# Expert outputs scattered to token order, FFN moved into its own batch's round, first preparation reordered

## The chip, the cores and the metric

The kernel runs on one core of a Trainium2 chip. The time is the device time of one execution in microseconds. Three executions of the kernel before took 855.63, 857.69 and 858.66 us; their median, 857.69 us, is what a new time is compared with.

## The reference

Input x has 8 batches of 512 tokens with 128 features. Two layers follow one another. The parts that matter here:

```python
# each layer: x = x + s * silu(moe or ffn), both from the layernormed xn
# layer 0: s = attention(xn), and the mixture of experts
normed = layernorm(hidden)                     # xf: (4096, 128)
top_idx = argmax(xf @ router_w)                # one of 8 experts per token
w = where(top_idx == e, sigmoid(max logit), 0)
routed += (silu(xe @ g) * (xe @ u)) @ d        # xe = xf * w, per expert
shared = silu(xf @ sh_gate) * (xf @ sh_up) @ sh_down
return hidden + routed + shared
# layer 1: s = state space model, and the FFN
xv = silu(conv(x @ W_in) + conv_b)
dt, B, C = split(xv @ W_x)
delta = softplus(dt @ W_dt + b_dt)
h[t] = exp(delta*A) * h[t-1] + delta * B * xv  # 16 states, scan over 512 tokens
y = (sum_n h * C + xv * D) @ W_out
ffn = (silu(xn @ w_gate) * (xn @ w_up)) @ w_down
out = x + y * silu(ffn)
```

## The kernel before, in words

All arithmetic is float32. The program has four blocks, one after another, and in each block every engine has its own list of instructions in program order, with semaphores between the engines. PE is TensorE, DVE is VectorE, ACT is ScalarE, POOL is GpSimd, SP issues plain DMAs.

**Block 1** (lines 142 to 465) normalises the tokens, finds each token's expert and a place (`pos`) for it in a list of 40 tiles of 128 slots, sorted by expert.

**Block 2** (lines 468 to 940) is attention with the shared expert, batch by batch, while POOL scatters the scaled tokens `nf_all` into `xs_dram` by `pos` (line 556). Then come the experts: for each of the 40 slot tiles SP loads 128 rows (four buffers `xs_t`), PE turns them, multiplies with the expert's weights, ACT and DVE make the hidden values, and SP stores the output tile `yt` to `ys_dram` (line 547), in slot order.

**Block 3 starts at line 943.** POOL first gathers the expert outputs back in token order, 32 indirect DMAs of 128 rows, each added onto `res_all` (line 1076). For batch i, `gates(i)` on ACT takes silu of that sum, and `residual(i)` on DVE multiplies it with attention's output, adds x and takes statistics; `moments(g)`, `roots(g)` and `norms(g)` normalise a group of batches (`GROUPS`, line 984), and `turn(i)` and `turned(i)` transpose them into `xn1T_all`.

Then the state space model runs in rounds, one batch each (`rounds`, line 1024). Round b scans batch b: in eight steps q, ACT writes the decays `dA` into PSUM banks 0 to 3 (line 1323), POOL writes the drives `dbx` = B times du (line 1158), DVE scans (line 1571, two scans per q), PE multiplies the states with `W_out` into banks 6 and 7, and DVE (twelve states) or ACT and POOL (four states) scale with C and sum up (lines 1587, 1360, 1090). In the same round the next batch b+1 is prepared: `conv_gate`, `ssm`, skip, C rows, `dt`, softplus (ACT: abs, relu, exp, ln; POOL: the sums, delta and du), and its FFN (`ffn_up`, `ffn_tanh`, `ffn_hidden`, `ffn_down`, `gate_tanh`, `gate`), all through PSUM banks 4 and 5; `x_in` and `conv_silu` start on batch b+2. The output of batch b-1 is put together on POOL.

The rounds of batch -1 (no scan) are written out by hand as `first_preparation` on PE, ACT and DVE: batch 0's preparation with its FFN, mixed with the gates, residuals and turns of the batches that are still arriving. Round 7, the last with scans, prepares nothing.

Where a helper issues the matmuls, their line is 1178.

Of the kernel before, what the change touches and what calls it, by code (L numbers as in the profile page):

```python
# [5 lines left out]
def attention_moe_mamba_ffn(nc, t, out):  # L6
# [13 lines left out]
    ds = bass.ds  # L20
# [22 lines left out]
    with ctx:  # L43
# [7 lines left out]
        xs_dram = nc.dram_tensor("xs_dram", [SLOT_TILES * P, D], fp32, kind="Internal").ap()  # L51
        ys_dram = nc.dram_tensor("ys_dram", [SLOT_TILES * P, D], fp32, kind="Internal").ap()
# [7 lines left out]
        nf_all = sb("nf_all", [P, NT, D])  # L60
# [81 lines left out]
        with ExitStack() as ph:  # L142
# [8 lines left out]
            zeros = sb1("zeros", [P, SLOT_TILES * D // 4])  # L151
# [25 lines left out]
            s_zd = sem("p1_slots_zeroed")  # L177
            s_ones = sem("p1_bv_ones")
# [18 lines left out]
            def _(sp):  # L197
# [21 lines left out]
            def _(pool):  # L219
                nc.gpsimd.memset(eps[:, :], LN_EPS).then_inc(s_eps, 1)  # L220
                nc.gpsimd.memset(bvb[:, :], 1.0).then_inc(s_ones, 1)
                nc.gpsimd.memset(zeros[:, :], 0.0).then_inc(s_zero, 1)
# [70 lines left out]
            def _(act):  # L293
# [23 lines left out]
                def scaled(b):  # L317
                    act.wait_ge(S["score"], b + 1)
                    act.wait_ge(S["nf_ps"], b + 1)
                    for i in tiles(b):  # L320
                        ins = nc.scalar.activation(nf_all[:, i, :], bank[bN[b % 2]][:, cols4(i)], ACT.Copy,
                                                   scale=score[:, i:i + 1])
# [23 lines left out]
            def _(dve):  # L346
# [59 lines left out]
                nc.vector.tensor_tensor(vobias[:, :], bank[bV][:, 0:D], rows[:, 0, :], ALU.add).then_inc(s_vob, 1)  # L406
                dve.wait_ge(s_std, 2)
# [60 lines left out]
        with ExitStack() as ph:  # L468
# [30 lines left out]
            xs_t = over[:, 0:UN * D].rearrange("p (u d) -> p u d", d=D)  # L499
# [5 lines left out]
            yt = over[:, 2560:2560 + UN * D].rearrange("p (u d) -> p u d", d=D)  # L505
            E = {n: sem("p4_" + n) for n in ("xT_ps", "xT", "gu_ps", "th", "ha", "hm", "hT_ps", "hT", "y_ps", "y")}
            s_in = [sem(f"p4_slots_loaded_{i}") for i in range(UN)]
            s_out = [sem(f"p4_slots_stored_{i}") for i in range(UN)]
# [9 lines left out]
            def _(sp):  # L518
# [14 lines left out]
                for u in range(UN):  # L533
# [14 lines left out]
                for u in range(UN):  # L548
                    sp.wait_ge(s_out[u], 16 * (SLOT_TILES // UN))
# [1150 lines left out]
```

## Time and profile before

| | |
|---|---|
| median of 3 executions | 857.69 us (855.63 to 858.66) |
| the profiled execution | 858.88 us |
| its span, first to last instruction | 857.0 us |
| PE, DVE, ACT, POOL busy | 674.9, 674.2, 485.3, 516.6 us |
| mean granted clock of TensorE | 0.928 of full speed |

The span is 1.9 us shorter than the execution's own time. Busy times are sums of instructions; a wait on a semaphore or the issue of a DMA from SP is not busy. A row of the timeline merges instructions of one kind that follow one another (x4: four of them). "Idle before" is how long the engine had stood, and the arrow names what ended it. The granted clock is 1.0 at 2.4 GHz and 0.5 at 1.2 GHz.

### The profile page before, as it was taken

Reading aid. Unit: us, or ns where it says so; the run is one execution under the profiler, and the core shown is the slowest. Engines: PE = TensorE matmul, PEld = TensorE weight load, DVE = VectorE, ACT = ScalarE, POOL = GpSimd, SP = SyncE. Lnnn points to the kernel's source line nnn. Section 1 sums busy time; section 2 is a strip of 40 time slices with the busy share of each in tenths; the row PEclk is TensorE's granted clock in tenths of the full one; section 3 lists DMA queues with packets and bytes.
Section 4 is the critical chain, followed back from the end, with each engine's and each line's share of the span. In section 5 each row is a group of like instructions: output and inputs, shape, how many; then the busy total and the mean of one; then the engine's idle time right before and its main releaser. Section 6 shows DMA issues by size and latency. Waiting matters only on the chain. (4 is left out here: it accounts for less than half of the span.)

```text
span 857.0 us, 13505 instructions
## 1 busy us (share of the span) xinstructions
PE 674.9 (79%) x3984; PEld 499.7 (58%) x3984; DVE 674.2 (79%) x1174; ACT 485.3 (57%) x946; POOL 516.6 (60%) x281
## 2 busy tenths in 40 slices
PE   1948999998999614335889899898798897988573
PEld 1934656665555401213577787777677776778573
DVE  6855786876666434274999999989999999999994
ACT  1625666665434223151785875956858668586561
POOL 1006610000000088662489999999899999999993
PEclk9968999999999956675999999999999999999998
DMA  7501100001222123520211320413203213142000
GB/s 220 199 10 47 44 15 0 0 12 55 56 64 68 47 31 37 130 98 0 100 50 50 117 71 27 161 50 109 77 26 135 74 42 136 34 137 75 12 2 13
DMA packets 45062, 56.41 MB, mean 66 GB/s; under 512 B 6344, under 2 KB 35536, under 8 KB 45008
## 3 DMA queue, kind: packets, MB, share of 16 engines
q1 hardware_dynamic: 37648, 51.00, 18.3%
q0 software_dynamic: 5632, 4.20, 2.7%
q10 hardware_dynamic: 1728, 0.57, 0.3%
q8 instruction: 24, 0.39, 0.2%
q14 instruction: 30, 0.25, 0.1%
HBM read 46.06 MB, written 9.70 MB: 65 GB/s over the span
## 5 line engine op out<-in xcount | busy, mean ns | idle before, releaser
L1571 DVE TENSOR_TENSOR_SCAN xnT_all<-psum,nfT_all 128x1024 f32<-128x1024 f32 x128 | 285.3, 2269 | 2.7 <-issue 2.7
L1178 PEld LDWEIGHTS psum<-W_out,xnT_all 128*128 128x128 f32 x2048 | 242.4, 196 | 40.4 <-issue 38.5
L1178 PE MATMUL psum<-W_out,xnT_all 128*128 128x128 f32 x2048 | 244.9, 279 | 18.7 <-DVE acc L1587 18.7
L1323 ACT ACTIVATE psum<-delta,A 128x511 f32<-128x511 f32 x256 | 163.2, 678 | 40.1 <-DVE xnT_all L1571 39.3
L1076 POOL DMA_INDIRECT res_all<-ys_dram,pos x32 | 50.3, 1572 | 196.3 <-issue 196.3
L1158 POOL TENSOR_TENSOR nfT_all<-nf_all,du 128x1024 f32<-128x1024 f32 x64 | 149.1, 2357 | 24.1 <-DVE xnT_all L1571 22.9
L1158 POOL TENSOR_TENSOR nfT_all<-attn_all,du 128x1024 f32<-128x1024 f32 x64 | 149.6, 2360 | 4.0 <-DVE xnT_all L1571 4.0
L1587 DVE SCALAR_TENSOR_TENSOR acc<-psum,Cc,acc 128x128 f32<-128x128 f32 x352 | 96.5, 339 | 7.8 <-PE psum L1178 7.8
L1178 PE MATMUL psum<-vo_all,wgu 128*128 128x512 f32 (+1 forms) x96 | 51.2, 660 | 43.9 <-DVE hff L1607 43.7
L556 POOL DMA_INDIRECT xs_dram<-nf_all,pos x32 | 31.9, 996 | 68.3 <-issue 57.5
L1178 PE MATMUL psum<-vo_all,W_taps 128*128 (+4 forms) x128 | 59.9, 615 | 0.7 <-ACT vo_all L1341 0.7
L1178 PEld LDWEIGHTS psum<-vo_all,wgu 128*128 128x128 f32 x96 | 17.1, 198 | 60.4 <-issue 46.8
L605 PEld LDWEIGHTS psum<-vo_all,PT 128*128 128x128 f32 x256 | 31.0, 191 | 23.5 <-ACT PT L750 17.6
L669 PE MATMUL psum<-gud,xnT_all 128*128 x80 | 43.6, 628 | 0.4 <-ACT xnT_all L785 0.4
L1360 ACT ACTIVATE ts<-psum,Cc 128x128 f32<-128x128 f32 x128 | 35.7, 356 | 10.1 <-PE psum L1178 10.1
L1178 PEld LDWEIGHTS psum<-vo_all,W_taps 128*128 128x128 f32 x128 | 24.4, 200 | 26.5 <-issue 25.4
L605 PE MATMUL psum<-vo_all,PT 128*128 (+1 forms) x256 | 36.9, 287 | 1.4 <-ACT PT L750 1.4
L909 DVE COPY xnT_all<-psum 128x256 f32<-128x256 f32 x40 | 17.0, 424 | 26.0 <-PE psum L681 26.0
L575 PE MATMUL psum<-k_w,q_w 128*128 128x512 f32 x64 | 34.4, 624 | 0.8 <-issue 0.8
L1603 DVE SCALAR_TENSOR_TENSOR fa<-tf,psum 128x512 f32<-128x512 f32 x24 | 15.9, 661 | 23.8 <-ACT tf L1371 23.8
L1178 PE MATMUL psum<-wd,hff 128*128 128x128 f32 x192 | 26.1, 298 | 9.4 <-DVE hff L1607 9.4
L1347 ACT ACTIVATE tconv<-psum,convb 128x512 f32<-128x512 f32 x16 | 10.9, 684 | 37.6 <-PE psum L1178 37.6
(189 smaller groups left out, 1163.7 us busy)
## 6 DMA issues: line engine op xcount, KB each, us to landing
nf_all<-bt_dram SPq DMA_DIRECT2D x32, 512.0 KB, 5.3
attn_all<-bt_dram SPq DMA_DIRECT2D x32, 512.0 KB, 3.6
xs_dram<-zeros SPq DMA_DIRECT2D x4, 640.0 KB, 7.5
xnT_all<-xs_dram SPq DMA_DIRECT2D x40, 64.0 KB, 1.9
ys_dram<-xnT_all SPq DMA_DIRECT2D x40, 64.0 KB, 1.5
x_all<-in_x_dram SPq DMA_DIRECT2D x8, 256.0 KB, 6.2
out_dram<-ow SPq DMA_DIRECT2D x8, 256.0 KB, 2.4
gud<-in_gate_dram SPq DMA_DIRECT2D x1, 1024.0 KB, 6.7
```

Of the source, the lines that this page charges most:

```text
L556: pool.indirect_dma_start(xs_dram, bass.IndirectOffsetOnAxis(ap=pos[:, i:i + 1], axis=0), nf_all[:, i, :], None).then_inc(s_sc, 16)
L575: nc.tensor.matmul(bank[j % 2], q_w[:, j * P:(j + 1) * P], k_w[:, :], start=True, stop=True)\
L605: ins = nc.tensor.matmul(bank[4][:, j * P:(j + 1) * P], PT[:, j % 2, c, :], vo_all[:, ds(b * TPB + c, 1), :], start=(c == 0), stop=(c == T ...
L669: nc.tensor.matmul(bank[2 + u % 2], xT[:, u % 2, :], gud_flat[:, ds(expert[u], 2 * I)], start=True, stop=True).then_inc(E["gu_ps"], 1)
L909: nc.vector.tensor_copy(hT[:, u % 2, :, :], bank[4 + u % 2][:, 0:KI * P].rearrange("p (k s) -> p k s", s=P))\
L1076: pool.indirect_dma_start(res_all[:, i, :], None, ys_dram, bass.IndirectOffsetOnAxis(ap=pos[:, i:i + 1], axis=0), compute_op=ALU.add).then ...
L1158: nc.gpsimd.tensor_tensor(dbx[:, i % R, :, :], B_pair(q), du[:, p, h:h + 1, :].to_broadcast([P, 2, L]), ALU.mult)\
L1178: return nc.tensor.matmul(o, l, r, start=start, stop=stop)
L1323: ins = nc.scalar.activation(dA[:, i % RA, k, 1:L], delta[:, p, h, 1:L], ACT.Exp, scale=A[:, h, 2 * q + k:2 * q + k + 1])
L1360: ins = nc.scalar.activation(ts[:, i, j, :], bank[Gb[n % 2]][:, j * P:(j + 1) * P], ACT.Copy, scale=Cc[:, p, j, n:n + 1])
L1571: nc.vector.tensor_tensor_scan(hring[:, i % R, :, :].rearrange("p n l -> p (n l)"), dA[:, i % RA, :, :].rearrange("p n l -> p (n l)"), dbx ...
L1587: nc.vector.scalar_tensor_tensor(acc[:, p, j, :], bank[Gb[m % 2]][:, j * P:(j + 1) * P], Cc[:, p, j, m:m + 1], acc[:, p, j, :] if i else s ...
```

## The change

**Experts' outputs.** A token's row in `xs_dram` gets a 129th word, its token number, written in block 1 (`token`, into the last column of `nf_rows`); the rows that fill up unused slots carry numbers of spare rows behind the last token. The output tiles are no longer stored by SP but scattered by POOL with these numbers into `moe_dram`, in token order, within the experts' stage. Block 3 then reads a batch's 512 rows with one plain DMA that adds onto `res_all`: 8 DMAs in place of 32 gathers. `xs_t` has eight buffers; the load of tile u+8 waits for the scatter of tile u.

**FFN.** All steps of batch b's FFN move from round b-1 to round b. The round before the first scan has none, and the last round gets one.

**First preparation.** On PE, ACT and DVE it is written in another order. Skip, C rows and the two dt products use banks 0 to 3, which hold the decays later (`bS, bC, bD`), so the zero columns of `dA` are set after them. The two softplus sums, delta and du of batch 0 move from POOL to DVE. The groups of batches are (0), (1, 2), (3 to 7) in place of (0), (1 to 3), (4 to 7); the variance takes six DVE operations in place of eight; silu's table is loaded ahead.

```diff
@@ block 1
+                link(nc.vector.tensor_scalar(token[:, :], thr, pid[:, 0:1], None, ALU.add))
+                nc.vector.tensor_copy(nf_rows[:, :, D].bitcast(u32), token[:, :])
...
@@ experts, SP
-                for u in range(SLOT_TILES):
-                    if u + UN < SLOT_TILES:
-                        sp.wait_ge(E["xT_ps"], u + 1)
-                        sp.dma_start(xs_t[:, u % UN, :], slots(xs_dram, u + UN)).then_inc(s_in[u % UN], 16)
-                    sp.wait_ge(E["y"], u + 1)
-                    sp.dma_start(slots(ys_dram, u), yt[:, u % UN, :]).then_inc(s_out[u % UN], 16)
...
+                for u in range(SLOT_TILES - XN):
+                    sp.wait_ge(E["xT_ps"], u + 1)
+                    sp.wait_ge(s_out[u % UN], 16 * (u // UN + 1))
+                    sp.dma_start(xs_t[:, u % XN, :], slots(xs_dram, u + XN)).then_inc(s_in[u % XN], 16)
@@ experts, POOL
+                for u in range(SLOT_TILES):
+                    pool.wait_ge(E["y"], u + 1)
+                    pool.wait_ge(s_in[u % XN], 16 * (u // XN + 1))
+                    pool.indirect_dma_start(moe_dram, bass.IndirectOffsetOnAxis(ap=xs_t[:, u % XN, D:ROW].bitcast(u32), axis=0),
+                                            yt[:, u % UN, :], None).then_inc(s_out[u % UN], 16)
@@ block 3, POOL
-                    for i in range(b * TPB, (b + 1) * TPB):
-                        pool.indirect_dma_start(res_all[:, i, :], None, ys_dram,
-                                                bass.IndirectOffsetOnAxis(ap=pos[:, i:i + 1], axis=0),
-                                                compute_op=ALU.add).then_inc(s_moe[b % 2], 16)
+                    pool.dma_start(res_all[:, b * TPB:(b + 1) * TPB, :],
+                                   moe_dram[b * L:(b + 1) * L, :].rearrange("(j p) d -> p j d", p=P),
+                                   accum_op=ALU.add).then_inc(s_moe[b % 2], 16)
@@ PE, first_preparation
                         ssm()
-                        skip()
-                        C_rows()
                         dt(0)
                         dt(1)
                         turn(1)
                         turn(2)
-                        ffn_up(0)
+                        skip()
+                        C_rows()
+                        pe.wait_ge(F["xT"], 2)
+                        x_in(b + 2, 0)
                         turn(3)
-                        ffn_up(1)
-                        ffn_up(2)
-                        ffn_down()
-                        x_in(b + 2, 0)
+                        turn(4)
                         x_in(b + 2, 1)
...
@@ DVE, rounds
-                        if prep and 3 <= q < 6:
+                        if scan and 3 <= q < 6:
                             ffn_hidden(q - 3)
...
-                        if prep and q == 6:
+                        if scan and q == 6:
                             gate()
```

How the instructions of an engine stand in the program, at the places that the prediction speaks of. In the names, `nf_all` and `nf_rows` are the same memory, which in block 3 holds B broadcast to all partitions.

POOL at the start of block 3, before (the gathers are all 32 of line 1076; here the first twelve and the last four), then the first preparation's sums:

```order
L1076 DMA res_all<-ys_dram,pos 128x128 x8
L1076 DMA res_all<-ys_dram,pos 128x128 [waits p5_gathered_0]
L1076 DMA res_all<-ys_dram,pos 128x128 x3
...
L1115 TENSOR_TENSOR lg<-lg,rl 128x1024 [waits p6_delta,p6_lg,p6_rl]
L1119 TENSOR_TENSOR e<-ab,e 128x1024 [waits p6_e1]
L1127 TENSOR_TENSOR delta<-e,lg 128x1024 [waits p6_dA,p6_du,p6_corr,p6_sp]
L1135 TENSOR_TENSOR du<-delta,xv 128x1024 [waits p6_dbx,p6_xv,p6_delta]
L1158 TENSOR_TENSOR nfT_all<-nf_all,du 128x1024 [waits p6_scan,p6_B_loaded_0,p6_du]
```

and now, from the last of the experts' scatters (`moe_dram` with `xnT_all`'s part `yt`) on:

```order
L575 DMA moe_dram<-xnT_all 5376x128 [waits p4_slots_loaded_7,p4_y]
...
L1095 DMA res_all<-moe_dram 128x4x128 x2
L1095 DMA res_all<-moe_dram 128x4x128 [waits p5_gathered_0]
L1095 DMA res_all<-moe_dram 128x4x128 [waits p5_gathered_1]
...
L1177 TENSOR_TENSOR nfT_all<-nf_rows,du 128x1024 [waits p6_scan,p6_B_loaded_0,p6_du]
```

The sums of batch 0 have left POOL, and its first work on data is the drives. DVE before the first scan, before (`fa`, `hff`, `G`: the FFN; `ts`: the normed rows):

```order
L1540 TENSOR_SCALAR var<-var 128x16 [waits p5_mv]
L1603 SCALAR_TENSOR_TENSOR fa<-tf,psum 128x512 [waits p6_hf,p6_tf]
L1607 SCALAR_TENSOR_TENSOR hff<-fa,psum 128x512 [waits p6_dn_ps,p6_fa]
...
L1613 SCALAR_TENSOR_TENSOR G<-tg,psum 128x512 [waits p6_og,p6_tg]
L1545 RECIPROCAL rs<-std 128x16 [waits p5_std]
L1552 TENSOR_SCALAR ts<-x_all,mean,rs 128x128 [waits p5_xT_ps,p5_rs]
```

and now:

```order
L1563 SCALAR_TENSOR_TENSOR var<-tmp,var 128x20 [waits p5_mv]
L1633 TENSOR_TENSOR lg<-lg,rl 128x1024 [waits p6_rl,p6_lg]
L1637 TENSOR_TENSOR e<-ab,e 128x1024 [waits p6_e1]
L1628 MEMSET psum 128x4 [waits p6_rl,p6_acc0,p6_C]
L1642 TENSOR_TENSOR delta<-e,lg 128x1024 [waits p6_corr,p6_sp]
L1647 TENSOR_TENSOR du<-delta,xv 128x1024 [waits p6_delta]
L1569 RECIPROCAL rs<-std 128x20 [waits p5_std]
L1576 TENSOR_SCALAR ts<-x_all,mean,rs 128x128 [waits p5_rs]
L1576 TENSOR_SCALAR ts<-x_all,mean,rs 128x128 x3
```

Four operations came in, three pairs of the FFN and its gate went out, and the last group of norms has 20 operations in place of 16. The third place is DVE in the last round, before, where a scan's pair is followed by sums alone:

```order
L1571 SCALAR_TENSOR_TENSOR xnT_all<-psum,nfT_all 128x1024 [waits p6_G,p6_dbx,p6_dA] x2
L1587 SCALAR_TENSOR_TENSOR acc<-psum,Cc,acc 128x128 [waits p6_acc,p6_G]
L1587 SCALAR_TENSOR_TENSOR acc<-psum,Cc,acc 128x128 [waits p6_acc] x3
L1571 SCALAR_TENSOR_TENSOR xnT_all<-psum,nfT_all 128x1024 [waits p6_G,p6_dbx,p6_dA] x2
L1587 SCALAR_TENSOR_TENSOR acc<-psum,Cc,acc 128x128 [waits p6_acc,p6_G]
```

and now, in the steps 3 to 5 (the gate follows in step 6):

```order
L1595 SCALAR_TENSOR_TENSOR xnT_all<-psum,nfT_all 128x1024 [waits p6_G,p6_dbx,p6_dA] x2
L1653 SCALAR_TENSOR_TENSOR fa<-tf,psum 128x512 [waits p6_hf,p6_tf]
L1657 SCALAR_TENSOR_TENSOR hff<-fa,psum 128x512 [waits p6_dn_ps,p6_fa]
L1611 SCALAR_TENSOR_TENSOR acc<-psum,Cc,acc 128x128 [waits p6_acc,p6_G]
L1611 SCALAR_TENSOR_TENSOR acc<-psum,Cc,acc 128x128 [waits p6_acc] x3
```

In the other rounds the FFN's operations stand where they stood, with another batch's number in their waits.

## Rows read from the trace of the kernel before

**Rows 1.** Busy time by stage: us, then PE, PEld, DVE, ACT, POOL, clock, DMA share, GB/s

```profile
212.00:296.00 84.00, 77.03 (x360) 45.57 (x360) 51.76 (x134) 33.26 (x121) 0.00 (x0) 1.00 0.22 61
...
296.00:417.00 121.00, 46.05 (x128) 23.72 (x128) 58.07 (x122) 42.65 (x59) 72.73 (x42) 0.65 0.25 53
...
694.00:749.00 55.00, 50.32 (x338) 40.36 (x337) 53.66 (x76) 39.95 (x72) 54.18 (x27) 1.00 0.25 83
...
803.00:857.00 54.00, 31.89 (x256) 30.57 (x255) 42.67 (x62) 20.91 (x44) 39.25 (x22) 0.93 0.03 10
...
304.00:336.00 32.00, 10.52 (x20) 4.60 (x20) 12.70 (x43) 9.69 (x12) 26.60 (x18) 0.61 0.29 35
```

**Rows 2.** Timeline of POOL, 300 to 361 us: start, duration, instruction, idle before

```profile
300.44 1.62 POOL L1076 DMA_INDIRECT res_all<-ys_dram,pos  x1 [186.84 <-issue]
...
306.06 1.54 POOL L1076 DMA_INDIRECT res_all<-ys_dram,pos  x1 [0.30 <-issue]
...
358.66 1.54 POOL L1076 DMA_INDIRECT res_all<-ys_dram,pos  x1 [0.30 <-issue]
```

**Rows 3.** Timeline of ACT, 300 to 400 us

```profile
309.37 1.28 ACT L1331 ACT_TABLE_LOAD   x1 [14.71 <-DMA res_all<-ys_dram,pos]
...
337.97 0.69 ACT L1347 ACTIVATE tconv<-psum,convb 128x512 f32<-128x512 f32 x1
...
358.43 0.63 ACT L1331 ACTIVATE xnT_all<-res_all 128x512 f32<-128x512 f32 x1 [10.18 <-DMA res_all<-ys_dram,pos]
...
366.51 1.28 ACT L1400 ACT_TABLE_LOAD   x1
...
367.80 1.06 ACT L1400 ACTIVATE ab<-ab 128x1024 f32<-128x1024 f32 x1
...
397.34 0.60 ACT L1371 ACTIVATE tf<-psum 128x512 f32<-128x512 f32 x1 [20.70 <-PE psum L1178]
```

**Rows 4.** Timeline of DVE, 330 to 420 us

```profile
332.42 0.69 DVE L1519 TENSOR_TENSOR xnT_all<-xnT_all,attn_all 128x512 f32<-128x512 f32 x1 [5.08 <-ACT xnT_all L1331]
...
340.25 3.16 DVE L1552 TENSOR_SCALAR ts<-x_all,mean,rs 128x128 f32<-128x128 f32 x12
...
382.79 0.18 DVE L137 TENSOR_TENSOR tmp<-tmp 128x16 f32<-128x16 f32 x1
...
389.83 2.26 DVE L1540 TENSOR_SCALAR var<-var 128x16 f32<-128x16 f32 x1
...
411.51 4.46 DVE L1571 TENSOR_TENSOR_SCAN xnT_all<-psum,nfT_all 128x1024 f32<-128x1024 f32 x2
...
417.14 4.47 DVE L1571 TENSOR_TENSOR_SCAN xnT_all<-psum,nfT_all 128x1024 f32<-128x1024 f32 x2
```

**Rows 5.** Timeline of POOL beside attention, one of the scatters

```profile
76.94 0.95 POOL L556 DMA_INDIRECT xs_dram<-nf_all,pos  x1 [1.53 <-DMA xs_dram<-nf_all,pos]
```

**Rows 6.** Waits in the experts' stage, 212 to 296 us: total, times, longest

```profile
PE psum L655 <- DMA xnT_all<-xs_dram: 2.0, 4, 0.8
```

**Rows 7.** Timeline of PE, 316 to 365 us

```profile
317.00 1.08 PE L1301 MATMUL psum<-const,ts 128*128 128x128 f32 x4 [22.65 <-DVE ts L1552]
...
318.77 9.44 PE L1178 MATMUL psum<-vo_all,W_taps 128*128 128x512 f32 x16 [0.69 <-ACT vo_all L1341]
...
340.13 3.63 PE L1178 MATMUL psum<-xv,W_x 128*40 128x512 f32 x4 [11.92 <-DVE xv L1597]
...
360.56 3.62 PE L1178 MATMUL psum<-ssmT,W_dt 128*128 128x512 f32 x4
```

**Rows 8.** Timeline of POOL, 382 to 393 us

```profile
382.79 9.27 POOL L1158 TENSOR_TENSOR nfT_all<-nf_all,du 128x1024 f32<-128x1024 f32 x4
```

**Rows 9.** Timeline of DVE, 767 to 791 us, a round's FFN

```profile
767.68 0.65 DVE L1603 SCALAR_TENSOR_TENSOR fa<-tf,psum 128x512 f32<-128x512 f32 x1
...
768.37 0.69 DVE L1607 SCALAR_TENSOR_TENSOR hff<-fa,psum 128x512 f32<-128x512 f32 x1
...
790.14 0.68 DVE L1613 SCALAR_TENSOR_TENSOR G<-tg,psum 128x512 f32<-128x512 f32 x1
```

More of the change, by code:

```diff
@@ L532, in _ @@
                 sp.wait_ge(s_sc, NT * 16)
-                for u in range(UN):
+                for u in range(XN):
                     sp.dma_start(xs_t[:, u, :], slots(xs_dram, u)).then_inc(s_in[u], 16)
@@ L989, in attention_moe_mamba_ffn @@
             rs1 = sb6("rs1", [P, NT])
+            eps1 = sb6("eps1", [P, 1])
             over = xnT_all[:, :]
@@ L1231, in dt @@
                         w("ssm", 1)
-                        if h:
+                        if h and scan:
                             w("C", 1)
-                        mm(bank[bM[h]], W_dt[:, h * P:(h + 1) * P], ssmT[:, :]).then_inc(S["dt_ps"], 1)
+                        mm(bank[bD[h]], W_dt[:, h * P:(h + 1) * P], ssmT[:, :]).then_inc(S["dt_ps"], 1)
                     def skip():
@@ L1451, in first_preparation @@
                         conv_silu(b + 2, 0)
+                        turned(3)
+                        turned(4)
                         conv_silu(b + 2, 1)
-                        for i in GROUPS[2]:
-                            turned(i)
+                        turned(5)
+                        turned(6)
+                        turned(7)
                     if prep and not scan:
@@ L1465, in round_ @@
                             scale_state(b, p, q - 3)
+                        if scan and 2 <= q < 5:
+                            ffn_tanh(q - 2)
+                        if scan and q == 5:
+                            gate_tanh()
                         if not prep:
@@ L1499, in _ @@
                 gates(3)
+                gates(4)
                 conv_silu(0, 0)
+                gates(5)
+                conv_silu(0, 1)
+                gates(6)
+                gates(7)
                 roots(1)
-                conv_silu(0, 1)
-                gates(4)
-                gates(5)
                 rounds(act, round_)
@@ L1590, in add_state, with conv_gate @@
                                                            ALU.mult, ALU.add).then_inc(S["acc"], 1)
[L1592 to L1598 removed]
+                    def conv_gate(h):
+                        if h == 0:
+                            w("acc_ps", 0)
+                            w("du", 0)
+                        w("yh", h + 1)
+                        nc.vector.scalar_tensor_tensor(xv[:, h, :], tc_[:, h, :], 1.0, bank[bM[h]],
+                                                       ALU.add, ALU.mult).then_inc(S["xv"], 1)
@@ new lines, in deltas, with drives @@
+                    def deltas():
+                        w("sp", 1)
+                        w("corr", 1)
+                        nc.vector.tensor_tensor(delta[:, 1 - p, :, :], e1[:, :, :], lg[:, :, :], ALU.add)\
+                            .then_inc(S["delta"], 1)
+                    def drives():
+                        w("delta", 1)
+                        nc.vector.tensor_tensor(du[:, 1 - p, :, :], delta[:, 1 - p, :, :], xv[:, :, :], ALU.mult)\
+                            .then_inc(S["du"], 1)
```

204 lines of the change are left out of this document (111 added, 93 removed).

## The prediction

> **What bounds the kernel now.** I read the stages first, then inside the one that no engine fills, engine by engine. The experts' stage (212 to 296) is PE's. The rounds (694 to 749) are DVE's and POOL's, with 53.7 and 54.2 us busy of 55; the last one (803 to 857) is lighter, since it prepares no next batch [rows 1]. Between them lie 121 us (296 to 417) in which DVE is busy 58 us and PE 46 us at 0.65 of its clock: a chain of waits, not work.
>
> In that stretch POOL issues 32 gathers from 300.4 to 360.2, one each 1.88 us [rows 2]. ACT works in program order, so its gate of batch 6 at 358.4 waits 10.2 us for a gather while the skip, the C rows and the softplus stand behind it [rows 3]. After that the shared FFN is in the way: its second tanh runs at 397.3 after 20.7 us of waiting [rows 3], because DVE was in small variance operations of 2.2 us each. The first scan starts at 411.5, the third at 417.1 [rows 4]. From there on the rounds repeat, so I follow the change to the third scan and then only to the end.
>
> **Part 1, before the experts.** Seven small DVE operations give the row numbers; one of such size takes 0.18 us [rows 4], with gaps 1.2 us in all, on DVE's path: +1.2. Rows of 516 B in place of 512 are scattered beside attention, whose scatters had some 100 us of room: 0.
>
> **Part 2, the experts' stage.** The store of each slot leaves SP and becomes an indirect scatter on POOL, which was idle there. A scatter takes 0.95 us, its pause 0.3, and it lands 1.5 later [rows 5]; a slot's step takes about 2.0 us (some 80 us for 40), and four output buffers give 8 us, so POOL keeps up and nobody waits for it. On SP the refill is no longer behind a store, and eight buffers replace four: it now waits for the scatter of the same slot (2.5 us after the output), with over three steps to spare. PE waited 2.0 us for loads, four times [rows 6]; with the irregular step behind each I take 3.0 back. The last scatter's issue is 0.6 longer than a store's (0.95 against some 0.35). POOL, which started at 300.4 [rows 2], starts at 300.4 + 1.2 - 3.0 + 0.6 = 299.2.
>
> **Part 3, the residual's input.** 32 gathers become eight plain accumulating DMAs of 256 KB. No row shows one. From below: the issue of one gather, 1.54 us, while the bytes need at least 2.2 us (35 GB/s kept 0.29 of the DMA engines busy [rows 1], so 121 GB/s is the most). From above: the same cost per row as a gather, 4 x 1.54 = 6.2 us. I take 3.0, nearer the lower end, because the rows need no index, and the gather's price contains one. A landing comes 1.8 us after an issue's end (307.6 [rows 2] to 309.4 [rows 3]), so batch 0 is there at t0 = 299.2 + 3.0 + 1.8 = 304.0. Up to 2.9 us a batch the chain below never waits for batch 7, needed at t0 + 20.4; at 3.0 it hardly does.
>
> The Trainium skill, DMA: Bandwidth & Descriptors, section Anatomy of one DMA, gives 2.0 us plus the bytes at 436 GB/s for such a DMA and calls descriptor generation small; by it t0 would be about 301.8, and the sum 2.2 us less. No row here has a direct one.
>
> **Part 4, the chain from t0 to the third scan.** All from rows; PE at its low level, since it idles between.
> - Gate, residual, variance, norm, turn: 9.4 us before (309.4 [rows 3] to 318.8 [rows 7]); less a table load moved ahead (1.28 [rows 3]) and two links of DVE, 7.6.
> - x_in, both halves: 9.4 [rows 7]. To t0 + 17.0.
> - conv_silu's two passes 1.4 [rows 3] and the gate's product 0.7 [rows 4]: 19.0.
> - ssm 3.6 [rows 7], copied out 0.6 [rows 3]: 23.3. The gates of 3 to 7 and their residuals (2.3 us each) fit on ACT and DVE beside x_in.
> - Both dt 3.6 [rows 7] and the second abs and relu 1.4: 28.2.
> - Exp, Ln, each with a table load, 2 x 2.35 [rows 3], then two passes of 1.06: 35.0.
> - ACT goes on with skip, C and two turned copies, then root and its table, until 38.5. DVE makes the sum, delta and du, no longer POOL: 128x1024 with two SBUF inputs is 1.2 us (0.69 for 512 columns, 0.18 for 16 [rows 4]), so three of them after ACT's last pass: 38.6. POOL had taken about 2.4 for each.
> - Now DVE has norms(2), 20 tensor_scalars (0.26 each, twelve in 3.2 [rows 4]), 5.3 us, and POOL starts four products of B and du, 9.3 us [rows 8], at the same moment. While those four ran before, a DVE operation over 16 columns took 2.26 us instead of 0.18 [rows 4], one per POOL operation. So I add the two: 14.6, and norms(2) ends at 53.2.
> - The first scan starts then. The third waits for a row of work on PE and ACT behind batch 4's norms (about 49): a turn 1.1 [rows 7], x_in's second half 4.7, conv_silu 1.4, the last turn with its copy and a bank's wait 2.5, two decays 1.3. Third scan at t0 + 60.0 = 364.0.
>
> Before it was 417.1, so this saves 53.1. Batch 0's FFN is not on this chain any more.
>
> **Part 5, the rounds.** FFN of batch b moves from round b-1 to round b, in the same slots; seven rounds hold one FFN as before. The last round gets one that it did not have. DVE is full there, so all of its work counts: 3 x (0.65 + 0.69) + 0.68 [rows 9] = 4.7 us. PE and ACT have room for theirs in a round with a full DVE, and do the same in the rounds before. The tail behind the last scan stays.
>
> **Sum.** 857.0 - 53.1 + 4.7 = 808.6 us of span. The profiled execution took 858.88 for 857.0 of span, 1.9 more: 810.5. The median of the runs, 857.69, is 1.2 below that execution; I forecast **809.5 us**. About 0.3%, 2.6 us, is what a measurement of this kernel can tell from no change.
>
> **The rivals.**
> - *The DMAs cost by the row* (6.2 us a batch). t0 is 3.2 later, and batch 7 comes 43.4 us after batch 0, not 20.4 at the latest: 23.0 more. 809.5 + 26.2 = 835.7. For it: scatter and gather both are priced 128 rows at a time, 0.95 and 1.54. Against: an index is part of both. Chance 0.2; a pitch of 4 to 5 us gives 817 to 826 and is in my case.
> - *DVE is not held by POOL in norms(2)*. Then it ends at 43.9, and the third scan is bound by x_in and the turns at about t0 + 54.3: 803.8. For it: twelve norms ran at 0.26 while gathers were issued. Against: those write descriptors only, and the row of 2.26 is itself a tensor_scalar. Chance 0.1.
> - *The scatters hold the experts*, which ends slower than before. POOL takes one slot after another; as soon as a scatter with its pause needs more than 2.0 us, every step takes that long, and from 2.0 + 48/40 = 3.2 us the whole gain is gone. At two gathers' issues and a pause, 3.4 us, it is 40 x 1.4 = 56 more: 866. Against: 32 scatters took 0.95 beside a DVE that was busy with one- and two-input operations [rows 5]. Chance 0.03.
> - *The FFN in the last round costs nothing or the shorter preparation is eaten in round 0*: the first would need DVE to idle there, and it doesn't; the second would need round 0 to lack something (B loads come 7 us after ssm, in time). Up to 10 us more, 0.04, inside the range.
>
> The Trainium skill, SBUF — State Buffer, section SBUF: two separate sides, says for the third rival that a DVE operation in a 2-port mode keeps GpSimd from writing descriptors, 3.1 us in place of 0.62 for such a DMA. By that rule the step would be at its edge, 3.1 to 3.4 us, and the time near 860. It would need such operations in the loop; the loop's three DVE operations read PSUM, and no row shows a scatter held.
>
> **How the numbers follow.** My case with its slower pitches, 801 to 826, has 0.65; the case by the row 0.2; DVE unheld 0.1; the rest slower still. The low end takes in DVE unheld together with the earlier t0, 800. The high end reaches a pitch of 5.7 us, 832. Faster by over 0.3%: 0.96, since even the case by the row is 22 us faster. Slower: 0.03. Same: 0.01.
>
> **What would show it.** In the profile after: POOL has 40 scatters between about 217 and 297 at 1 us; eight DMAs end by 325; the first scan starts near 357 and the third near 364, with DVE's norms(2) at 2.3 us for the first few of them; DVE shows fa, hff and G in the last round, which grows by 4.7 us. I am wrong in the size if POOL's eight issues last over 3 us each, or if ACT waits for a DMA after the gate of batch 2; wrong in the mechanism if the third scan is early but the rounds after it are longer than the 55 us of before; wrong in the sign only if the experts' stage grows from 84 us to over 130.

## The result, and the profile after

The changed kernel takes 814.1 us (median of 4 runs, 812.6 to 815.2) against 856.7 us before (854.9 to 858.7): ratio 0.950, 95% interval 0.947 to 0.953, so 5% faster. The forecast was 809.5 with a range of about 800 to 832. In the profiled executions the span went from 857.0 to 811.8 us, 45.2 less; the sum of the prediction had 48.4.

Busy time by stage, with the columns of [rows 1] (experts, preparation, round 0, round 6, last round with the end):

```profile
212.00:292.00 80.00, 75.85 (x358) 45.21 (x358) 51.26 (x133) 32.94 (x120) 38.06 (x40) 1.00 0.21 60
300.00:365.00 65.00, 31.83 (x94) 16.00 (x95) 49.46 (x115) 37.26 (x54) 24.08 (x14) 0.74 0.45 98
363.00:419.00 56.00, 50.36 (x327) 39.30 (x327) 52.04 (x70) 39.94 (x68) 46.17 (x21) 0.97 0.22 76
695.00:750.00 55.00, 46.81 (x328) 40.57 (x327) 53.58 (x76) 37.89 (x67) 54.26 (x27) 0.94 0.25 83
750.00:812.00 62.00, 42.26 (x300) 37.05 (x298) 48.45 (x73) 24.24 (x50) 40.39 (x23) 0.88 0.03 9
```

Between the experts and the third scan lie 74 us (291 to 365) where 121 had been, and in the last 65 of them DVE is busy 49. POOL has 38 us of work in the experts' stage and nobody waits for it. The row for 694 to 749 in [rows 1] is round 5, so round 6 is compared by its third scans: 53.8 us from 697.2 to 751.0 now, 53.5 from 749.1 to 802.6 before. From the last round's third scan to the end there are 60.8 us where 54.4 had been. Timeline of POOL, the end of the experts and the residual's input:

```profile
291.40 0.96 POOL L575 DMA_INDIRECT moe_dram<-xnT_all  x1 [0.78 <-ACT xnT_all L817]
303.96 2.76 POOL L1095 DMA_DIRECT2D res_all<-moe_dram  x2 [11.60 <-issue]
308.81 1.28 POOL L1095 DMA_DIRECT2D res_all<-moe_dram  x1 [2.09 <-DMA res_all<-moe_dram]
...
320.22 1.28 POOL L1095 DMA_DIRECT2D res_all<-moe_dram  x1 [0.59 <-DMA res_all<-moe_dram]
```

Against [rows 2]: eight issues of 1.3 to 1.4 us in place of 32 of 1.54, the last over at 321.5. But the first starts at 303.96, later than the first gather did (300.44). POOL's last scatter was issued by 292.4; then 11.6 us pass. Timeline of ACT:

```profile
290.85 0.28 ACT L817 ACTIVATE xnT_all<-psum 128x128 f32<-128x128 f32 x1 [1.46 <-PE psum L712]
300.11 1.28 ACT L1333 ACT_TABLE_LOAD   x1 [8.98 <-PEq L483]
...
308.54 0.63 ACT L1351 ACTIVATE xnT_all<-res_all 128x512 f32<-128x512 f32 x1 [6.94 <-DMA res_all<-moe_dram]
...
335.46 1.06 ACT L1422 ACTIVATE ab<-ab 128x1024 f32<-128x1024 f32 x1
```

From the end of the last output's copy (291.13) to block 3's first instruction 9.0 us go by. Before the change it was 2.2, from 294.66 to 296.88, by the timelines of ACT and DVE of the kernel before:

```profile
294.38 0.28 ACT L798 ACTIVATE xnT_all<-psum 128x128 f32<-128x128 f32 x1 [1.46 <-PE psum L693]
...
296.88 0.48 DVE L1509 MEMSET ssmT<- 128x512 f32 x1 [3.53 <-PEq L468]
```

The gate of batch 0, 308.54, is the prediction's t0. The softplus's exp runs at t0 + 27. Timeline of DVE after the change:

```profile
343.54 1.23 DVE L1647 TENSOR_TENSOR du<-delta,xv 128x1024 f32<-128x1024 f32 x1
...
344.99 13.30 DVE L1576 TENSOR_SCALAR ts<-x_all,mean,rs 128x128 f32<-128x128 f32 x20
358.21 4.46 DVE L1595 TENSOR_TENSOR_SCAN xnT_all<-psum,nfT_all 128x1024 f32<-128x1024 f32 x2
...
364.90 4.47 DVE L1595 TENSOR_TENSOR_SCAN xnT_all<-psum,nfT_all 128x1024 f32<-128x1024 f32 x2 [1.05 <-ACT psum L1343]
371.33 1.13 DVE L1611 SCALAR_TENSOR_TENSOR acc<-psum,Cc,skip_sb 128x128 f32<-128x128 f32 x4 [1.97 <-PE psum L1192]
```

The third scan came at 417.1 [rows 4] and now comes at 364.9, 52.2 us earlier. The norms took 13.3 us for 20 (forecast 14.6). Timeline of PE:

```profile
315.96 8.99 PE L1192 MATMUL psum<-vo_all,W_taps 128*128 128x512 f32 x16 [0.69 <-ACT vo_all L1361]
327.14 1.91 PE L1192 MATMUL psum<-xv,W_x 128*40 128x512 f32 x4 [2.20 <-DVE xv L1621]
330.56 1.98 PE L1192 MATMUL psum<-ssmT,W_dt 128*128 128x512 f32 x4 [1.51 <-ACT ssmT L1399]
...
363.99 3.47 PE L1192 MATMUL psum<-xv,W_x 128*40 128x512 f32 x4 [0.95 <-DVE xv L1621]
...
796.93 5.44 PE L1192 MATMUL psum<-W_out,xnT_all 128*128 128x128 f32 x32 [3.49 <-DVE acc L1611]
```

The ssm and dt of batch 0 run at a granted clock of 1.00 (1.91 and 1.98 us), where [rows 7] has 3.6 each at 0.50. PE had idled 2.20 and 1.51 us before them, and 11.92 before that ssm of the kernel before. The last two lines show the opposite: the ssm of round 0 at 0.52 and the last projections at 0.69. The same work before, both at 1.00:

```profile
417.29 1.88 PE L1178 MATMUL psum<-xv,W_x 128*40 128x512 f32 x4 [2.01 <-DVE xv L1597]
...
843.66 3.81 PE L1178 MATMUL psum<-W_out,xnT_all 128*128 128x128 f32 x32 [2.62 <-DVE acc L1587]
```

### The profile page after: what moved, and what is told of

It reads as the page before. It is cut to its first block and busy times, and to the rows that moved or that the text cites. A ratio compares the mean times of both kernels' runs of the same rounds, so it can differ in the third digit from the quotient of the medians.

```text
span 811.8 us, 13548 instructions
## 1 busy us (share of the span) xinstructions
PE 667.7 (82%) x3984; PEld 495.1 (61%) x3984; DVE 671.3 (83%) x1180; ACT 482.2 (59%) x944; POOL 504.8 (62%) x293
## 5 line engine op out<-in xcount | busy, mean ns | idle before, releaser
L1177 POOL TENSOR_TENSOR nfT_all<-nf_rows,du 128x1024 f32<-128x1024 f32 x64 | 149.3, 2362 | 33.0 <-DVE du L1647 23.3
L575 POOL DMA_INDIRECT moe_dram<-xnT_all x40 | 38.4, 960 | 141.3 <-ACT xnT_all L817 141.3
L568 POOL DMA_INDIRECT xs_dram<-nf_rows,pos x32 | 31.4, 981 | 68.1 <-issue 56.1
L1192 PE MATMUL psum<-vo_all,wgu 128*128 128x512 f32 (+1 forms) x96 | 48.2, 625 | 26.8 <-DVE hff L1657 26.8
L1192 PE MATMUL psum<-vo_all,W_taps 128*128 (+4 forms) x128 | 62.4, 635 | 7.1 <-ACT vo_all L1361 7.1
L624 PEld LDWEIGHTS psum<-vo_all,PT 128*128 128x128 f32 x256 | 31.0, 191 | 23.6 <-ACT PT L769 17.6
L1380 ACT ACTIVATE ts<-psum,Cc 128x128 f32<-128x128 f32 x128 | 35.8, 359 | 13.4 <-PE psum L1192 13.2
L1109 POOL TENSOR_TENSOR accP<-accP,ts 128x512 f32<-128x512 f32 x16 | 20.4, 1272 | 18.0 <-ACT ts L1380 18.0
L1321 PE MATMUL psum<-const,ts 128*128 128x128 f32 x32 | 5.9, 333 | 30.6 <-DVE ts L1576 29.4
```

The lines of the kernel that those rows point to most:

```text
L568: pool.indirect_dma_start(xs_dram, bass.IndirectOffsetOnAxis(ap=pos[:, i:i + 1], axis=0), nf_rows[:, i, :], None).then_inc(s_sc, 16)
L575: pool.indirect_dma_start(moe_dram, bass.IndirectOffsetOnAxis(ap=xs_t[:, u % XN, D:ROW].bitcast(u32), axis=0), yt[:, u % UN, :], None).the ...
L624: ins = nc.tensor.matmul(bank[4][:, j * P:(j + 1) * P], PT[:, j % 2, c, :], vo_all[:, ds(b * TPB + c, 1), :], start=(c == 0), stop=(c == T ...
L1109: nc.gpsimd.tensor_tensor(accP[:, :, :], ts[:, 0, :, :] if i == 1 else accP[:, :, :], ts[:, i, :, :], ALU.add).then_inc(S["accP"], 2 if i ...
L1177: nc.gpsimd.tensor_tensor(dbx[:, i % R, :, :], B_pair(q), du[:, p, h:h + 1, :].to_broadcast([P, 2, L]), ALU.mult)\
L1192: return nc.tensor.matmul(o, l, r, start=start, stop=stop)
```

## The experiments

**The parts alone.** Three kernels take the change apart. The first has the scatters and the plain DMAs only:

```diff
-sp.dma_start(slots(ys_dram, u), yt[:, u % UN, :]).then_inc(s_out[u % UN], 16)
+pool.indirect_dma_start(moe_dram, bass.IndirectOffsetOnAxis(ap=xs_t[:, u % XN, D:ROW].bitcast(u32), axis=0),
+                        yt[:, u % UN, :], None).then_inc(s_out[u % UN], 16)
...
-    pool.indirect_dma_start(res_all[:, i, :], None, ys_dram,
+pool.dma_start(res_all[:, b * TPB:(b + 1) * TPB, :],
```

> The kernel before with the scatters to token order and the eight plain DMAs alone; the FFN and the first preparation stay as they were. Theory: the path of before waits for gathers at the gates of batches 3 to 6, so block 3's start moves little, the ssm that started at 340.1 comes near 329 and the second dt's abs that ended at 365.5 comes near 338; the FFN in the way stays as long as it was. The third scan, 417.1 before, comes near 390, and the time near 830 us. Rival: the waits behind the FFN (20.7 us at its second tanh) swallow the earlier start, third scan after 405 and the time above 845.

Measured 834.1 us, ratio 0.972 (0.970 to 0.975). Timeline of its DVE:

```profile
390.00 4.47 DVE L1589 TENSOR_TENSOR_SCAN xnT_all<-psum,nfT_all 128x1024 f32<-128x1024 f32 x2
397.49 1.13 DVE L1605 SCALAR_TENSOR_TENSOR acc<-psum,Cc,skip_sb 128x128 f32<-128x128 f32 x4 [3.02 <-PE psum L1196]
```

The third scan is where the theory put it, 27.1 us earlier, but the median is only 23.6 lower. Round 0 accounts for 1.6 of the difference (57.2 us from third scan to third scan for 55.6): its ssm took 3.40 us instead of 1.88, and DVE's first accumulation waited 3.0 us for PE instead of 1.4. Another 1.2 is that the profiled execution of the kernel before, whose 417.1 is compared, ran 1.2 above its median; the rest is below 1 us.

The second kernel has the rest: the FFN and the preparation as changed, the gathers as before.

> The changed kernel with the old gathers: SP stores the slots, 32 indirect gathers fill the residual's input; FFN and preparation as changed. Theory: the last gather lands near 362, ACT's ssm copy now stands behind the gate of batch 7, so the softplus starts near 370, the first scan near 395 and the third near 401; with 4.7 us for the last round's FFN the time is near 846 us. So both parts alone give 27 and 11 us, together 43: the gathers hide half of what the new order gives. Rival: the parts add up, this one gives 16 us or more, time under 841.

Measured 846.5 us, ratio 0.987 (0.984 to 0.990), third scan at 397.4 (401 expected). The two parts give 23.6 and 11.2 us, 34.8 together, and the whole change 42.6. The third kernel moves the FFN alone (`ffn_up`, `ffn_tanh`, `ffn_hidden`, `gate` count b in place of b + 1, and go out of the first preparation).

> The kernel before with the FFN of each batch moved to the round of its own scans and nothing else. Theory (DVE's norms are held one per POOL operation while POOL's softplus sums and products run): third scan near 400 in place of 417.1, last round 4.7 longer, time near 845 us. If the norms are not held: third scan near 391, time 836. Rival: the FFN in the preparation cost nothing because something else ends at the same time, then the time is 857.7 + 4.7 = 862.

Measured 846.9 us, ratio 0.986 (0.983 to 0.990). Timeline of its DVE:

```profile
373.79 16.91 DVE L1547 TENSOR_SCALAR ts<-x_all,mean,rs 128x128 f32<-128x128 f32 x16
390.63 4.45 DVE L1566 TENSOR_TENSOR_SCAN xnT_all<-psum,nfT_all 128x1024 f32<-128x1024 f32 x2
...
396.19 4.45 DVE L1566 TENSOR_TENSOR_SCAN xnT_all<-psum,nfT_all 128x1024 f32<-128x1024 f32 x2
```

Sixteen norms took 16.9 us beside POOL's sums and products, and 4.2 before the change, when POOL was idle:

```profile
407.40 4.19 DVE L1552 TENSOR_SCALAR ts<-x_all,mean,rs 128x128 f32<-128x128 f32 x16
```

So the case with the norms held is the one that holds. The FFN alone gives as much as FFN and preparation together do while the gathers are there (10.8 and 11.2): behind late input the reordered preparation earns nothing that these times resolve. No kernel has the scatters and the FFN without it, so how much of the 7.8 us by which the whole exceeds its parts belongs to the preparation, and how much to the FFN alone, is not shown.

**The end of the experts' block.** The 9.0 us after the last output were in no term of the prediction. First, POOL issues the DMAs of batches 0 and 1 in the experts' block, behind its wait for the last scatters:

```diff
 for u in range(UN): pool.wait_ge(s_out[u], 16 * (SLOT_TILES // UN))
+pool.wait_ge(S["res"], at(NB - 1, "res", 1))
+for b in range(2):
+    pool.dma_start(res_all[:, b * TPB:(b + 1) * TPB, :],
+                   moe_dram[b * L:(b + 1) * L, :].rearrange("(j p) d -> p j d", p=P),
+                   accum_op=ALU.add).then_inc(s_moe[b % 2], 16)
...
-for b in range(NB):
+for b in range(2, NB):
```

> The changed kernel, with POOL issuing the plain DMAs of batches 0 and 1 in the experts' block, right behind its wait for the last scatters. From the last output (290.9) to block 3's first instruction 9 us pass, 2.2 before the change. Theory: the scatters' semaphores are there by 293.5 and the end of POOL's block costs the rest; the two DMAs are then issued at 293.5 to 296.3, the block ends 6 to 7 us behind the last of them (near 303), and the gate of batch 0 runs at block 3's start, 303 to 304 in place of 308.5; time 809 us. Rival: the last scatters land late; the DMAs are issued only at 299 to 300, the block ends at 303 without a further wait, the gate at 304 to 305.

```profile
292.70 0.96 POOL L576 DMA_INDIRECT moe_dram<-xnT_all  x1 [0.78 <-ACT xnT_all L823]
295.64 2.75 POOL L582 DMA_DIRECT2D res_all<-moe_dram  x2 [1.98 <-DMA moe_dram<-xnT_all]
309.10 2.58 POOL L1099 DMA_DIRECT2D res_all<-moe_dram  x2 [10.70 <-issue]
```

POOL's timeline settles the first question: the scatters' semaphores are there 2.0 us after the end of the last issue, so the landing is not what is late. But the block then ended at 305.3, 6.9 us after the two DMAs' issue, and the gate ran at 306.7, not at 303 to 304. 813.1 us, ratio 0.949 (0.946 to 0.952): not distinguishable from the changed kernel. The theory was right that the landing is not the cause and wrong about the gain: the end of the block moved back with the two DMAs.

Then the kernel before with additional indirect scatters by POOL: one behind the last output (its edit is shown), one behind the 28th (the number 28 in place of 40), and one behind each of the 40 with a single wait behind them all.

```diff
+pool.wait_ge(E["y"], 40)
+pool.indirect_dma_start(aside, bass.IndirectOffsetOnAxis(ap=pos[:, 0:1], axis=0), vo_all[:, 0, :], None).then_inc(s_aside, 16)
+pool.wait_ge(s_aside, 16)
```

> The kernel before with one more indirect scatter of 128 rows by POOL behind the last expert output, to a tensor that nobody reads. Theory: a scatter shortly before the end of POOL's block makes that end 6 to 7 us late: from the last output to block 3's first instruction 9 us in place of 2.2, as in the changed kernel, and the time near 864. Rival: the scatter's own issue and landing (0.7 + 1.0 + 1.5 us) is all: 3.5 us from the output, time near 859.

> The same, with the added scatter behind the 28th output, some 24 us before the last. Theory: what costs is the short time since the last scatter; POOL's end of block is over long before the other engines' and the time is that of before, 857. Rival: the cost is paid at the common end whenever POOL issued an indirect DMA late in the block: time near 863.

> The kernel before with 40 more indirect scatters of 128 rows by POOL, one behind each expert output, to tensors that nobody reads (nothing of the kernel itself is left out). With one such scatter behind the last output, block 3's first instruction came 2.6 us after its landing (6.3 after the last output); in the changed kernel, with 40, 5.8 us after (9.0 after the last output). Theory: the end of POOL's block grows with the number of indirect DMAs issued in it, 72 here as in the changed kernel: 9.0 us from the last output. Rival: it is something else of the changed kernel (longer rows, other waits on SP), and this one shows 6.3 again.

The last output's copy (ACT) ended at 291.64, 293.35 and 295.68. Block 3's first instruction (DVE) in each of the three, one behind the last, one behind the 28th, and 40:

```profile
297.98 0.48 DVE L1515 MEMSET ssmT<- 128x512 f32 x1 [7.66 <-PEq L469]
```

```profile
295.59 0.48 DVE L1515 MEMSET ssmT<- 128x512 f32 x1 [3.56 <-PEq L469]
```

```profile
304.73 0.48 DVE L1516 MEMSET ssmT<- 128x512 f32 x1 [10.36 <-PEq L469]
```

That is 6.3, 2.2 and 9.0 us. One scatter just before the end costs 4.1 us more than none (by the 2.0 us above it had landed 3.7 us after the output); one that is 24 us old costs nothing; 40 make it 9.0, the same as in the changed kernel, with none of its other edits. So the unexpected 6.8 us belong to the scatters on POOL, not to row length or SP's waits. Each of the three kernels was executed once: 858.1, 857.7 and 869.5 us. The forecast 864 for the first was too high by 6. In that execution the experts' first copy came 3.4 us earlier (209.2 against 212.6, ahead of any edit) and the experts took 0.4 more, so that block 3 began only 1.1 later than before; its third scan was yet 2.5 earlier (414.6 against 417.1), which was not explained. What happens in the microseconds before block 3 was not resolved; the trace of the changed kernel shows no instruction and no DMA traffic between 293.3 and 300.1.

The other part of the gap is POOL's own: it gives out its semaphore increments ahead of the first DMA.

```diff
-for n, per in names.items(): pool.sem_inc(S[n], 2 * per)
 for b in range(NB):
+    if b == 2:
+        for n, per in names.items(): pool.sem_inc(S[n], 2 * per)
```

> The changed kernel, with POOL issuing the first two plain DMAs ahead of its 40-odd semaphore increments in block 3. Theory: the increments take the 3.8 us between the block's start (300.1) and the first DMA (304.0), so the first DMA is at 300.2, the gate of batch 0 at 304.8, and the whole chain behind it 3.7 us earlier: 810.4 us. Rival: some engine waits for an increment in that time, or the gap is the block's entry on POOL and stays: within 1 us of 814.

```profile
300.44 2.75 POOL L1095 DMA_DIRECT2D res_all<-moe_dram  x2 [8.24 <-POOLq L483]
305.25 1.28 POOL L1095 DMA_DIRECT2D res_all<-moe_dram  x1 [2.06 <-DMA res_all<-moe_dram]
```

The gate of batch 0 came at 304.99 and the median 809.8 us, ratio 0.945 (0.942 to 0.947). So 3.5 us of the chain were 39 increments, instructions that count as no work in a profile. The whole chain did not keep them. DVE's timeline has the first scan 3.6 us earlier and the third 2.0:

```profile
362.92 4.47 DVE L1595 TENSOR_TENSOR_SCAN xnT_all<-psum,nfT_all 128x1024 f32<-128x1024 f32 x2 [2.42 <-ACT psum L1343]
```

That scan waited 2.4 us for ACT's decays, behind the second half of x_in, which took 5.74 us on PE where it had taken 4.16. The ssm that follows then took 1.91 us for 3.47, and round 0 was 54.3 us for 56.2 (third scan to third scan).

**The norms beside POOL.** POOL waits for all norms before its first product of round 0:

```diff
 pool.wait_ge(S["du"], at(b, "du", 1))
+if not end: pool.wait_ge(F["xn"], NB)
```

> The changed kernel, with POOL waiting for all of DVE's norms before its first product of B and du in round 0. Theory: the 20 tensor_scalars that took 13.3 us beside four POOL products take 0.26 each, 5.3 in all, when POOL is idle; the first scan comes at 352.6 in place of 358.2 and the third near 358.5 in place of 364.9; time 808 us. Rival A: the norms are slow by themselves (their inputs or outputs), they still take 13 us, and the time grows by 5 to 9 us. Rival B: the norms are faster, but POOL has lost its lead of products and round 0 becomes POOL's: it grows from 56.3 to 60 or more us and the time is within 2 us of 814.

```profile
344.82 5.21 DVE L1578 TENSOR_SCALAR ts<-x_all,mean,rs 128x128 f32<-128x128 f32 x20
...
352.62 4.61 DVE L1597 TENSOR_TENSOR_SCAN xnT_all<-psum,nfT_all 128x1024 f32<-128x1024 f32 x2 [2.58 <-issue]
...
358.32 4.46 DVE L1597 TENSOR_TENSOR_SCAN xnT_all<-psum,nfT_all 128x1024 f32<-128x1024 f32 x2
```

DVE's timeline has the same twenty operations in 5.2 us in place of 13.3, and the scans within 0.2 us of the forecast. Time 811.4 us, ratio 0.946 (0.942 to 0.950), an interval that overlaps the changed kernel's (0.947 to 0.953). By the profiled executions 3.5 of the 6.6 us are left; the rest came back as a longer round 0 and a longer round 3 (56.3 us for 54.7), where DVE waited 3.0 us for PE's projections in place of 1.4, behind an ssm of 3.51 us for 1.91. Rival B had the direction, but the round it gave 60 us has 57.0 (from conv gate to conv gate; 56.3 in the changed kernel).

The middle way lets POOL make one product first, together with the DMAs ahead of the increments:

```diff
 pool.wait_ge(S["scan"], at(b, "scan", i + 1 - R))
+if not end and i == 1: pool.wait_ge(F["xn"], NB)
```

> The changed kernel with two edits together: POOL issues the first two plain DMAs ahead of its semaphore increments, and in round 0 it makes one product of B and du, then waits for DVE's norms, then goes on. Theory: the gate of batch 0 is at 305.0, du ends near 341.3; one norm is held 2.3 us by the one product, the other 19 take 0.26 each, so the norms end at 348.7 and the first scan starts there; the third is near 357.5; POOL has one product more in hand than when it waited for all norms, so round 0 is no longer than 56.3. Time near 807. Rival: each product that POOL lacks at the first scan comes back as a wait in round 0 (57.0 there with none in hand), and the time stays at 809 to 810, what the first edit gave alone.

807.3 us, ratio 0.942 (0.940 to 0.944). DVE's timeline:

```profile
343.38 7.17 DVE L1578 TENSOR_SCALAR ts<-x_all,mean,rs 128x128 f32<-128x128 f32 x20
350.47 2.28 DVE L1597 TENSOR_TENSOR_SCAN xnT_all<-psum,nfT_all 128x1024 f32<-128x1024 f32 x1
...
356.52 4.46 DVE L1597 TENSOR_TENSOR_SCAN xnT_all<-psum,nfT_all 128x1024 f32<-128x1024 f32 x2
```

One product costs the norms one hold: 7.2 us. The chain up to du ran 1.9 us later than assumed, so the first scan came at 350.5 and not at 348.7; the third, 356.5, was 1.0 earlier than forecast. The last of this group keeps both edits and moves the norms of three batches to ScalarE:

```diff
+nc.vector.scalar_tensor_tensor(nm1[:, c], mean1[:, c], -1.0, rs1[:, c], ALU.mult, ALU.mult)
+nc.scalar.activation(xn1[:, i % 4, j, :], x_all[:, k, :], ACT.Identity, bias=nm1[:, k:k + 1], scale=rs1[:, k:k + 1])
```

> The same two edits, and the norms of batches 5 to 7 are made by ScalarE (x times the reciprocal root plus a bias that DVE computes), right behind its first decays; POOL waits after its first product for DVE's norms of batches 3 and 4 only. Theory: ScalarE is not held by POOL, 12 of its passes over 128 columns take 0.28 each as its output copies do; DVE's 8 norms end near 346, first scan 346, the third waits for ScalarE's copies and x_in's second half and comes near 356; time near 805. Rival: ScalarE becomes the bound of the stretch, the third scan comes after 358, and the time is that of the kernel with all norms on DVE or more.

807.2 us, ratio 0.941 (0.939 to 0.943), no better. DVE's timeline, then ACT's:

```profile
345.18 2.24 DVE L1589 SCALAR_TENSOR_TENSOR nm<-mean,rs 128x20 f32<-128x20 f32 x1
347.35 2.13 DVE L1598 TENSOR_SCALAR ts<-x_all,mean,rs 128x128 f32<-128x128 f32 x8
...
360.56 4.47 DVE L1617 TENSOR_TENSOR_SCAN xnT_all<-psum,nfT_all 128x1024 f32<-128x1024 f32 x2 [2.78 <-ACT psum L1347]
```

```profile
349.92 1.64 ACT L1369 ACTIVATE ts<-x_all,nm,rs 128x128 f32<-128x128 f32 x4
```

ScalarE needs 0.41 us a norm, not the 0.28 assumed, and the third scan waits for it and comes at 360.6, not 356: the rival's case. While it did so POOL was at work on its products (from 349.6 on). One operation over 20 columns was held for 2.24 us by POOL's product while eight norms without a product beside them took 2.13 together. The Trainium skill, SBUF — State Buffer, section SBUF: two separate sides, names which DVE operations contend with GpSimd for a shared port pair: those in a 2-port mode, and those with two SBUF inputs beside a GpSimd operation that reads SBUF; ScalarE never waits for it. The rows here agree as far as they go: the one held for 2.24 us has two SBUF inputs, and the scans, with one input in PSUM, take 2.27 to 2.29 us with POOL at work. The norms run from SBUF to SBUF and are held; that they do so in a 2-port mode is shown by no row.

**TensorE's clock.** The kernel with one product ahead of the norms (807.3 us), with work for PE that nobody reads in two gaps:

```diff
+for k in range(2): mm(bank[Gb[0]], ident, xn1T_all[:, 0:L])      # round 0, ahead of ssm
+for k in range(3): mm(bank[bM[0]], ident, xn1T_all[:, 0:L])      # last round, ahead of the last two projections
```

> The kernel with the two edits (DMAs ahead of the increments, one product ahead of the norms), and TensorE given work that nobody reads in two gaps: two matmuls over 512 columns (1.9 us) ahead of round 0's ssm, and three (2.8 us) ahead of the last two projections. Theory: in those places TensorE ran at its low level because it had idled before them: round 0's ssm took 3.3 to 3.6 us where TensorE was granted 0.52 and 1.9 where 1.0 was granted, and the last 32 matmul records 5.44 in every kernel with the FFN in the last round (idle 3.49 before) and 3.81 in those without (idle 2.62). With the gaps filled they take 1.9 and 3.8, round 0 is 1.5 shorter than 56.0 and the last part 1.6 shorter: time 804.5 us against 807.3. Rival: the added matmuls only push back the ssm and the projections, or the level stays low whatever runs there: time 807 to 809.

```profile
354.41 3.48 PE L1194 MATMUL psum<-vo_all,const 128*128 128x512 f32 x4 [0.69 <-ACT vo_all L1368]
357.83 2.06 PE L1194 MATMUL psum<-xv,W_x 128*40 128x512 f32 x4
...
787.27 2.74 PE L1194 MATMUL psum<-vo_all,const 128*128 128x512 f32 x6
790.92 3.81 PE L1194 MATMUL psum<-W_out,xnT_all 128*128 128x128 f32 x32 [0.91 <-DVE acc L1618]
```

805.7 us, ratio 0.940 (0.938 to 0.942). At the end the projections took 3.81 us as in the kernels without that round's FFN. The expectation says that every kernel with it showed 5.44, which is one too many: the kernel with norms on ScalarE idled 3.49 us there and took 3.81. So the 3.81 here fits the theory without proving it. In round 0 the added matmuls themselves ran low: the ssm started 1.8 us after the conv gates' end (356.0), where it had followed within 0.2, and though it then took 2.06, nothing was gained (a round of 56.45 us from conv gate to conv gate against 56.03). The end is 1.7 us shorter (59.1 us from the last round's third scan for 60.8), but round 3 is 1.6 longer (56.3 for 54.7), with its ssm at 2.93 us for 1.91, so the two profiled executions differ by 0.1 us (spans 804.1 and 804.2). The step over the kernel without them (0.942) is not resolved by the times; 1.0% over the changed kernel (0.950) is. This kernel has the lowest median of all the versions tried.

## Why the prediction was right, point by point

**Part 1 and 2, up to block 3.** The seven operations took 1.4 us (1.2 forecast). Where the experts start varies by 3.9 us between executions of the same code (first copy at 208.9 to 212.8 in six kernels that share it), which hides it. From the first slot's copy to the end of the last output's the old code needs 82.1 us in the trace of before (81.9 to 82.8 in the six) and the changed kernel 79.5, so 2.6 less for the 3.0 forecast; the waits of [rows 6] are gone. A scatter took 0.96 us for the 0.95 of [rows 5], with pauses in which POOL waited for the next output, so the rival of the held experts never came near. The forecast's reason, that the loop's DVE operations read PSUM, agrees with 40 equal issues; no run put an SBUF-only operation into the loop to test it.

**The step that failed** is in part 2: "The last scatter's issue is 0.6 longer than a store's". It took the end of the block for the issue alone. It was 9.0 us where 2.2 had been, 6.8 more. From 300.4, the experts start 1.0 earlier and take 2.6 less, the end of the block adds 6.8 and the way from it to the first DMA 0.3: POOL starts at 303.96 and not at 299.2.

**Part 3.** An issue lasts 1.3 to 1.4 us, not 3.0, and lands 3.2 after its end, not 1.8: together 4.6 for the forecast's 4.8. Both were mis-sized, the sum was not, and that is luck. The lower bound was misread too: the 121 GB/s come from one stretch, and other rows of [rows 1] give more by the same division (61 GB/s at 0.22 are 277). The median from issue to landing of the eight is 4.5. The Trainium skill, DMA: Bandwidth & Descriptors, section Anatomy of one DMA, gives 2.0 us plus bytes at 436 GB/s, 2.6 for the two together; the measurement decides against it for an accumulating DMA of 256 KB. One issue waits for the landing of the one two before it, which makes the pitch 2.3 us on average (from 303.96 to 320.22 for seven). The rival "by the row" would have wanted 6.2.

**Part 4, from t0.** Measured against forecast: x_in starts at t0 + 7.4 (7.6); ssm copied out 22.0 (23.3); abs and relu done 25.6 (28.2); softplus 32.4 (35.0); du 36.2 (38.6); norms 13.3 (14.6); first scan 49.7 (53.2); third 56.4 (60.0). The 3.6 us are 2.4 up to du and 1.3 in the norms. The first come mostly from ssm and dt, taken from rows at PE's low level and run at its high one (3.3 together, of which waits for ACT and DVE took some back), the second from the hold: four norms of 2.3 with the 16 others at 0.26 make 13.4, where adding both in full counts four norms twice. So t0 was 4.5 too early, the chain 3.6 too long, and the third scan at 364.9 met the forecast 364.0 by two errors of opposite sign.

**Part 5.** The FFN's seven DVE operations in the last round sum to 4.7 us, exactly as priced. Two things were left out. In round 0 DVE waits 0.6 us longer for PE (1.97 for 1.37), behind an ssm of 3.47 us for 1.88. And from the last round's third scan to the end there are 60.8 us for 54.4, so 6.4 more and not 4.7. "The tail behind the last scan stays" is wrong: with the FFN in that round PE's idle time before the last projections is 3.49 us for 2.62, and the projections take 5.44 for 3.81 at a granted clock of 0.69 for 1.00. The five kernels without that FFN idle 2.62 there and then take 3.81. Eight with it and without added matmuls idle 3.48 to 3.49; seven of them then take 5.44 and one, with norms on ScalarE, 3.81. So the low level is likely after that gap, not certain.

**Sum.** Third scan -52.2, round 0 +0.6, rounds 1 to 5 -0.3, round 6 +0.3, from the last round's third scan to the end +6.4: -45.2 us of span. Forecast: -53.1 + 4.7 = -48.4, which by its own terms is a time of 809.3. The time came out 4.6 above 809.5, inside the range. The upper part of the range stood for slower pitches of the DMAs, which did not happen; what happened was the block's end and PE's clock, which no term had, so that hit is luck as well. Of the rivals, "DVE is not held" is refuted by the norms of 13.3 us in three kernels and 16.9 in a fourth, and of 5.2 where POOL waits.

## What to carry to other kernels

- When two parts of a change share a chain, price them together: 23.6 and 11.2 alone were 42.6 together.
- Count what ends a block and what a queue does before its first DMA. Scatters by POOL just before the end of a block cost 4 to 7 us here, 39 semaphore increments 3.5, and neither is busy time.
- Where DVE works from SBUF beside POOL's two-input operations, a short order by hand (one product, then DVE's batch, then the rest) gave as much (807.3 us) as handing part of the work to a third engine that was already in the chain (807.2).

## What the runs showed that was not expected

- The end of a block after indirect DMAs on POOL: 2.2 us with none for 24 us, 6.3 with one just before, 9.0 with 40; 6.9 us behind the issue of two plain ones. The dependence on number is from two points, and each of the kernels with added scatters was executed once. Whether it is the number in the block or the number still fresh was not tried.
- PE's clock after a gap is not a matter of the gap alone: the ssm behind 2.01 us of idle time took 1.88 us in one kernel and 3.40 in another; what PE had done earlier differed between them, and no run separates it. Two matmuls put into the gap at 354.4 ran low themselves. At the end of the kernel the same gap of 3.49 us was followed by 5.44 us in seven kernels and 3.81 in one. In which round the ssm runs low differs from kernel to kernel: round 0 took 56.2 to 58.1 us in eight kernels where it was 3.3 to 3.6 us, 54.3 to 55.6 in four where it was 1.9, and 57.2 to 57.5 in the two between (2.1 and 2.3).
- An accumulating plain DMA of 256 KB needs 4.6 us from issue to the waiting engine and 1.3 to 1.4 to issue, for four times the rows of an accumulating gather, whose issue takes 1.54.
